# Where the score maxima are turned, constant stack rows, weight products, tables and padding rows in a macaron layer (two routed expert layers around one linear attention)

## The chip, the cores and the metric

The kernel runs on one core of one Trainium2 chip. The metric is the device time of one execution in microseconds (us). The kernel before was run three times: 2488.42, 2490.47 and 2494.25 us, median 2490.47 us.

## The reference

The input x has 8 batches of 512 tokens of 256 numbers (float32). Three sub-layers follow each other: an expert layer, a linear-attention layer, and the same expert layer again with the same weights.

```python
x = x + 0.5 * ffn(layernorm(x))
x = x + attention(layernorm(x))
x = x + 0.5 * ffn(layernorm(x))

def ffn(hs):                       # D = 256, 16 heads, 8 experts, top 2
    Q, K, V = hs@q_w+q_b, hs@k_w+k_b, hs@v_w+v_b      # 8 of each head's numbers are used
    attn = softmax(Q @ K.T / sqrt(8)); ao = attn @ V  # per batch and head, 512 x 512
    mla = ao @ o_w + o_b
    probs = softmax(mla @ router_w + router_b); topw, topi = top_k(probs, 2)
    h1 = gelu(mla @ w1[e] + b1[e]); h2 = h1 @ w2[e] + b2[e]
    return hs + 0.3 * sum over the two chosen e of weight * h2
```

The change lies in the expert layer, which runs twice; the attention layer between and the final combination are as they were.

## The kernel before

**Stages.** `load_and_make` loads small weights. Then `attend_and_apply_experts` runs for the first expert layer (tag f1), `attention_pass` (la), `attend_and_apply_experts` again (f2), and `combine` (fc). Each expert layer is three blocks with a barrier at the end of each: `attend_and_route` (softmax attention, router, and the scatter of each token's row into its two experts' regions of a DRAM table), `tile_tables` (21 VectorE steps that work out which expert each of 71 tiles belongs to, and beside them SP's load of the first half of w2 and of b2), and `experts` (71 tiles of 128 rows through w1, gelu and w2, with the second half of w2 loaded in its slot 1).

**Turns.** `attend_and_route` runs 11 turns over 8 batches, as a software pipeline. In one turn batch e has its scores, exponentials and weighted sums made ("e"), batch s = e+1 has its scores made once more to find row maxima ("s"), batch f = e+2 goes through the front (layer norm, q, k, v, "f"), and batch p = e-1 through the router and the scatter ("p"). The first turn has only f, the second s and f, the third e, s and f, turns 4 to 8 all four; the ninth has no f, the tenth e and p, the eleventh p alone. Turns 4 to 7 are in a hardware loop of two iterations with two turns each (`run_turns`), the others are written out. A turn has 16 groups (g = 0 to 15) of 4 score tiles; each engine's program is written out in this order, with front and router steps at fixed groups (tables FRONT and POST of each engine).

**The maxima.** Scores are computed from stacked bfloat16 parts: QS and KS hold, for every head, 6 products of parts in rows 0 to 47, zeros in rows 48 to 95, and in rows 96 to 98 the negated maxima (in QS) against ones (in KS). `score_for_max` (L749) makes a tile in one of three PSUM banks (SCM); VectorE's `maximum` (L501) reduces it. After 32 of the 64 tiles `split_maxima` (L508 to L511, four small VectorE operations) cuts the half's maxima into three parts, TensorE's `turn_maxima` (L758) turns them in the next SCM slot, and VectorE's `evacuate_mT` (L516) copies them out. The first half is split after g7 and turned after g8. The second half is split after g15 and turned at the very end of the turn. SP's `maxima` (L259, L261) writes them to DRAM, waits for that to land, and reads them back into rows 96 to 98; `score` (L768) of the next turn waits for it, for half 0 at its first tile and for half 1 at its 33rd.

**SP's order in a turn.** SP issues in program order: store of the residual, load of the next x, stores of the q and k parts (L276, L278), `maxima(s, 0)`, `stack_half(f, 0)`, `maxima(s, 1)`, `stack_half(f, 1)`. A `stack_half` (L253) is 12 DMAs of 64 KB, 8 partitions each, which lay the parts of half of the heads of batch f into QS and KS. It waits until the score tiles of batch e that read the same buffer are made. `score_for_max` of the next turn waits at its first tile for all 12 DMAs of half 0 (`half_loaded[0]`), and at its 33rd for those of half 1. TensorE works in order, so nothing behind such a wait runs.

**Beginnings.** GpSimd clears QS and KS and sets the ones with three memsets per buffer (`prepare_stacks`, L310, L311, L314), the first buffer before its part in the first turn, the second behind it. GpSimd also splits q and k into parts (`split`, L342 to L345, eight operations). In f1 TensorE multiplies o_w into w1 between turns one and two (`fold_weights`, L821 and L827, 8 experts), ScalarE evacuates.

**Ends.** After the last turn GpSimd's scatter of 8 indirect DMAs is followed by 8 more that write zero rows behind each expert's region (L386); then come the barrier, `tile_tables`, and another barrier.

Of the kernel before, what the change touches and what calls it, by code (L numbers as in the profile page):

```python
# [48 lines left out]

LN_STEPS = 6  # L50
# [33 lines left out]
def region_rows(tokens):  # L84
    return tokens + P


def attend_and_route(nc, new_sem, tag, nth, x_in, xr_out, xs, bank, ident, tri, w, scratch, routing, dims,
                     fold):
# [16 lines left out]
    K_MAX = 96  # L106
# [10 lines left out]
    PER_UNIT = SC + HALVES  # L117
# [3 lines left out]
    ROW, CW, start_row = routing["ROW"], routing["CW"], routing["start_row"]  # L121
# [4 lines left out]

    def max_slot(half):


        return (half + 1) * PER_HALF + min(HQ, SC - (half + 1) * PER_HALF) + half  # L130

    def score_slot(i):
        return i + sum(1 for half in range(HALVES) if i >= (half + 1) * PER_HALF + HQ)

    with ExitStack() as ctx:
# [38 lines left out]
        pad_f, pad_i = sb("pad_f", [P, E]), sb("pad_i", [P, E], I32)  # L174
# [12 lines left out]
        m3_ready, mT_filled = sem("m3_ready"), sem("mT_filled")  # L187
# [11 lines left out]
        dve_pads, carried, rows_out = sem("dve_pads"), sem("carried"), sem("rows_out")  # L199
# [5 lines left out]
        N_INIT = 9  # L205
        INIT = N_INIT * (nth + 1)

        SCE, SIDE, PVB, SCM = bank[0:2], bank[2:4], bank[4], bank[5:8]

        def run_turns(eng, turn, after_first=None, after_second=None, after_third=None):  # L210
            turn(None, None, START, None)
            if after_first is not None and fold is not None:
                after_first()
            turn(None, START, START + 1, None)
            if after_second is not None and fold is not None:
                after_second()
            turn(START, START + 1, START + 2, None)
            if after_third is not None and fold is not None:
                after_third()

            full = B - 3
            with eng.Fori(0, full // 2) as k:
                for odd in range(2):
                    b = k * 2 + (START + 1 + odd)
                    turn(b, b + 1, b + 2, b - 1, (START + 1 + odd) % 2)
            for b in range(START + 1 + full // 2 * 2, END + 1):
                turn(b if b < END else None, b + 1 if b + 1 < END else None,
                     b + 2 if b + 2 < END else None, b - 1)
# [6 lines left out]

        block = ctx.enter_context(nc.Block())

        @block.sync
        def _(sp):
# [3 lines left out]
            def stack_half(a, half, par, free):  # L243
# [20 lines left out]
            def turn(e, s, f, p, par=None):  # L264
                par_s, par_f = parity(s, 1, par), parity(f, 0, par)
# [15 lines left out]
                if f is not None:  # L281
                    if e is None:

                        sp.wait_ge(init, INIT if s is not None else INIT - 3)
# [9 lines left out]
            run_turns(sp, turn)  # L294
# [8 lines left out]
        def _(pool):  # L303
# [3 lines left out]

            def prepare_stacks(i, done):

                pool.memset(QS[i][0:K_MAX, :, :], 0.0).then_inc(init, 1)  # L310
                pool.memset(KS[i][0:K_MAX, :, :], 0.0).then_inc(init, 1)  # L311

                pool.wait_ge(init, INIT - N_INIT + done + 2)
                pool.memset(KS[i][K_MAX:K_EXP, :, :], 1.0).then_inc(init, 1)  # L314
                pool.wait_ge(init, INIT - N_INIT + done + 3)

# [3 lines left out]
            prepare_stacks(0, 3)  # L320
# [15 lines left out]
            def split(a):  # L336

                s = Steps(pool, pool_front, a, 6)
                wait(pool, split_stored, a * 32)
                for whole, rest, parts, ready, done in ((qf, qres, q3, q_ready, q3_ready), (kf, kres, k3, k_ready, k3_ready)):  # L340
# [23 lines left out]
            def turn(e, s, f, p, par=None):  # L364
# [5 lines left out]
                if s is None and p is None:  # L370

                    prepare_stacks(1, 6)

            def complete_biases():

# [7 lines left out]

            pool.wait_ge(pads_ready, nth + 1)
# [1548 lines left out]
```

## Time and profile before

| | |
|---|---|
| median of three runs | 2490.47 us |
| the profiled execution | 2496.27 us, its span 2494.6 us |
| f1: attend_and_route | from 14.0 us; first score tile at 79.1 us |
| f1: tables and experts | tables from 677.7 us, experts from 687.2 us |
| f2: attend_and_route | from 1523.4 us; first score tile at 1580.5 us |
| f2: tables | from 2184.0 us |
| busy, of the span | TensorE 79%, VectorE 62%, ScalarE 38%, GpSimd 26% |

Times are from the start of the span. A busy share is an average over stages: in the turns TensorE is busy about nine tenths of the time and VectorE over eight tenths, while at the starts and ends of the expert layers most engines wait. The profiled execution is 5.8 us above the median of the runs.

### The profile page before, as it was taken

Reading aid. Unit: us, or ns where it says so; the run is one execution under the profiler, and the core shown is the slowest. Engines: PE = TensorE matmul, PEld = TensorE weight load, DVE = VectorE, ACT = ScalarE, POOL = GpSimd, SP = SyncE. Lnnn points to the kernel's source line nnn. Section 1 sums busy time; section 2 is a strip of 40 time slices with the busy share of each in tenths; the row PEclk is TensorE's granted clock in tenths of the full one; section 3 lists DMA queues with packets and bytes.
Section 4 is the critical chain, followed back from the end, with each engine's and each line's share of the span. In section 5 each row is a group of like instructions: output and inputs, shape, how many; then the busy total and the mean of one; then the engine's idle time right before and its main releaser. Section 6 shows DMA issues by size and latency. Waiting matters only on the chain. (4 is left out here: it accounts for less than half of the span.)

```text
span 2494.6 us, 43922 instructions
## 1 busy us (share of the span) xinstructions
PE 1965.2 (79%) x12512; PEld 1086.7 (44%) x12513; DVE 1541.0 (62%) x3524; ACT 938.1 (38%) x1694; POOL 656.6 (26%) x674
## 2 busy tenths in 40 slices
PE   3898988898289959888889874599989898369940
PEld 2323333332079945655656563123333332069940
DVE  3688878885244436656666663588878885244433
ACT  1056556567122214322333321046555567212210
POOL 7422333221312231111100004522332321312246
PEclk9799999999689978888897886589998999779975
DMA  4333323220122231111011001332323230032236
GB/s 123 58 62 57 62 54 61 51 49 11 68 98 73 73 129 35 52 52 53 18 40 47 27 18 34 71 63 56 62 55 59 48 57 11 26 131 73 70 116 189
DMA packets 154273, 155.20 MB, mean 62 GB/s; under 512 B 19744, under 2 KB 144416, under 8 KB 153760
## 3 DMA queue, kind: packets, MB, share of 16 engines
q1 hardware_dynamic: 122912, 108.39, 19.1%
q0 software_dynamic: 10752, 26.23, 3.4%
q10 hardware_dynamic: 20448, 18.62, 2.1%
q8 instruction: 77, 1.26, 0.2%
q14 instruction: 84, 0.69, 0.1%
HBM read 90.80 MB, written 62.39 MB: 61 GB/s over the span
## 5 line engine op out<-in xcount | busy, mean ns | idle before, releaser
L501 DVE TENSOR_REDUCE f_M<-bank 128x1 f32<-128x512 f32 x1024 | 666.6, 684 | 222.1 <-PE bank L749 201.9
L435 ACT ACTIVATE f_PT<-bank 128x512 f32<-128x512 f32 x1024 | 574.9, 596 | 341.2 <-PE bank L768 330.7
L749 PE MATMUL bank<-f_KS,f_QS 96*128 96x512 bf16 x1024 | 424.8, 417 | 111.0 <-DVE f_M L501 79.3
L768 PE MATMUL bank<-f_QS,f_KS 99*128 99x512 bf16 x1024 | 402.5, 397 | 29.6 <-ACT f_PT L435 21.9
L778 PE MATMUL bank<-f_PT,f_V 128*32 128x512 f32 x2048 | 282.7, 627 | 0.0
L768 PEld LDWEIGHTS bank<-f_QS,f_KS 99*128 99x128 bf16 x1024 | 101.1, 100 | 395.6 <-ACT f_PT L435 268.3
L749 PEld LDWEIGHTS bank<-f_KS,f_QS 96*128 96x128 bf16 x1024 | 103.1, 101 | 262.7 <-DVE f_M L501 186.7
L1064 PE MATMUL bank<-f_w,f1m_gT 128*128 x568 | 136.2, 383 | 0.1
L1064 PE MATMUL bank<-f_w,f2m_gT 128*128 x568 | 135.9, 382 | 0.1
L357 POOL DMA_INDIRECT routed_rows<-f_AO,f_rows_i x128 | 124.2, 970 | 42.1 <-issue 42.1
L331 POOL TENSOR_TENSOR f_xr<-f_hs,f_half 128x1024 f32<-128x1024 f32 x16 | 30.3, 1893 | 301.7 <-DVE f_hs L81 268.8
L1064 PEld LDWEIGHTS bank<-f_w,f1m_gT 128*128 128x128 f32 x568 | 103.6, 193 | 11.8 <-issue 0.5
L1064 PEld LDWEIGHTS bank<-f_w,f2m_gT 128*128 128x128 f32 x568 | 103.6, 193 | 11.8 <-issue 0.5
L1000 ACT ACTIVATE f1m_gT<-f1m_hb 128x512 f32<-128x512 f32 x71 | 44.7, 630 | 158.8 <-DVE f1m_hb L1021 158.8
L1000 ACT ACTIVATE f2m_gT<-f2m_hb 128x512 f32<-128x512 f32 x71 | 44.7, 630 | 158.4 <-DVE f2m_hb L1021 158.4
L354 POOL TENSOR_TENSOR f_pool_carrier<-f_zero 128x1 f32<-128x1 f32 x16 | 3.1, 193 | 384.0 <-DVE f_rows_i L603 343.8
L1588 PE MATMUL bank<-la_o,la_attT 128*128 128x256 f32 x256 | 81.4, 473 | 16.1 <-ACT la_attT L1389 16.1
L1327 POOL TENSOR_TENSOR la_pool_carrier<-la_zero 128x1 f32<-128x1 f32 x8 | 1.5, 192 | 332.6 <-DVE la_idx L1418 332.6
L988 POOL COPY f1m_w1t<-folded_w 128x512 f32 x71 | 43.6, 614 | 170.8 <-PE bank L1053 154.1
L988 POOL COPY f2m_w1t<-folded_w 128x512 f32 x71 | 43.6, 614 | 170.4 <-PE bank L1053 154.0
L1516 DVE SCALAR_TENSOR_TENSOR la_sqk<-la_qk,la_low 128x512 f32<-128x512 f32 x64 | 41.4, 688 | 68.8 <-ACT la_low L1368 68.3
L1381 ACT ACTIVATE la_SS<-la_SS 128x512 f32<-128x512 f32 x32 | 20.1, 630 | 161.1 <-DVE la_SS L1463 161.1
(279 smaller groups left out, 3272.1 us busy)
## 6 DMA issues: line engine op xcount, KB each, us to landing
f_QS<-q_parts SPq DMA_DIRECT2D x192, 64.0 KB
f_KS<-k_parts SPq DMA_DIRECT2D x192, 64.0 KB
expert_rows<-f1m_y ACTq DMA_DIRECT2D x71, 128.0 KB, 1.7
expert_rows<-f2m_y ACTq DMA_DIRECT2D x71, 128.0 KB, 1.7
xr<-f_xr SPq DMA_DIRECT2D x16, 512.0 KB, 3.0
f_w<-in_L_ffn_w SPq DMA_DIRECT2D x4, 2048.0 KB, 8.2
q_parts<-f_q SPq DMA_DIRECT2D x16, 384.0 KB, 2.5
k_parts<-f_k SPq DMA_DIRECT2D x16, 384.0 KB, 2.5
```

The lines of the kernel that those rows point to most:

```text
L331: pool.tensor_tensor(XR[:, :, :], HS[:, :, :], half[:, :].unsqueeze(2).to_broadcast([P, T, D]), ALU.mult).then_inc(xr_half, 1)
L357: pool.indirect_dma_start(out=xs, out_offset=bass.IndirectOffsetOnAxis(ap=rows_i[:, t, n:n + 1], axis=0), in_=AO[par][:, t, :], in_offset= ...
L435: act.activation(PT[:, i % 8, :], SCE[i % 2][:, :], ACT.Exp).then_inc(probs_ready, 1)
L501: dve.tensor_reduce(M[:, t, h:h + 1], SCM[n % 3][:, :], AX.X, ALU.max).then_inc(scm_drained, 1)
L749: pe.matmul(SCM[n % 3][:, :], QS[par][0:K_MAX, h, t * P:(t + 1) * P], KS[par][0:K_MAX, h, :], start=True, stop=True).then_inc(scm_filled, 1)
L768: pe.matmul(SCE[i % 2][:, :], KS[par][0:K_EXP, h, t * P:(t + 1) * P], QS[par][0:K_EXP, h, :], start=True, stop=True).then_inc(sce_filled, 1)
L778: pe.matmul(PVB[hq * PV_W:(hq + 1) * PV_W, :], V[par][:, t, head(q, hq), :], PT[:, i % 8, :], start=(t == 0 and q % 2 == 0), stop=(t == T ...
L988: pool.tensor_copy(W1[:, buf, :], w["w1"][:, ds(e * F, F)]).then_inc(w1_ready, 1)
L1000: act.activation(GT[:, buf, :, :], Hb[:, buf, :, :], ACT.Gelu).then_inc(gT_ready, 1)
L1064: last = pe.matmul(OB[buf][:, 0:D], GT[:, buf, f, :], w["w2"][:, ds(e * (FC * D) + f * D, D)], start=(f == 0), stop=(f == FC - 1))
L1516: dve.scalar_tensor_tensor(sqk[par][:, i, :], qk[par][:, i, :], 0.0, low[:, i % 2, :], ALU.max, ALU.add).then_inc(sqk_ready, 1)
L1588: last = pe.matmul(OB[:, 0:D], attT[:, c, :], w["la_o"][:, c, :], start=(c == 0), stop=(c == KC - 1))
```

## The change

`attend_and_route` takes over the tables (`make_tables`) and the early load of w2; the block `tile_tables` is gone.

1. **Maxima.** Three small pieces spread over groups. Of batch s, half 0 is split at g12 (one of the four operations after each tile), turned after g13 and copied out at g14. Half 1 is left to the next turn, where the batch is e: split at g0, turned after g3, copied out at g4. Both use PSUM bank SIDE[1] in place of an SCM bank. `score_for_max` counts plain tiles.
2. **SP's order.** `maxima(e, 1)` stands first in a turn, `maxima(s, 0)` after the stores of q and k parts as before, then `stack_half(f, 0)` and `stack_half(f, 1)`.
3. **No loop.** All turns are written out.
4. **Constant rows.** ScalarE's queue issues, for each of two buffers, two DMAs that fill rows 48 to 95 from an SBUF row of zeros (about 0.79 MB each) and one that fills the ones. The memsets are gone. The 16 small loads of q_b move from SP's queue to ScalarE's.
5. **First batch.** q is split by VectorE, k by GpSimd; the KS half of the first stack (12 DMAs) is issued from ScalarE's queue.
6. **Weight products.** One expert's product at each even group of turn two and its bias products at each odd one, evacuated by ScalarE in the same groups.
7. **Ends.** Zero rows by plain DMAs, four from SP and four from ScalarE. The tables follow on VectorE in the same block, while GpSimd scatters. All of w2 (4 MB) is loaded by SP after turn three, b2 in slot 1 of `experts`, and `experts` waits for both.

```diff
@@ attend_and_route, constants
-    A_FRONT, A_SCM, A_POST = LN_STEPS, 3 * HALVES, 2 + 22
+    A_FRONT, A_SCM, A_POST = LN_STEPS, 3, 2 + 22
+    G_LAST, G_FIRST = 0, 12
@@ sync
                 for n, (i, j) in enumerate(TERMS):
...
-                    for to, source in ((QS[par], q_scr[i]), (KS[par], k_scr[j])):
+                    both = ((QS[par], q_scr[i]), (KS[par], k_scr[j]))
+                    for to, source in both[:1] if a == START else both:
@@
             def maxima(a, half, par):
-                sp.wait_ge(scm_drained, a * PER_UNIT + max_slot(half) + 1)
+                sp.wait_ge(mT_ready, a * HALVES + half + 1)
@@
             def turn(e, s, f, p, par=None):
+                if e is not None:
+                    maxima(e, 1, par_e)
                 if f is not None:
...
                 if s is not None:
                     maxima(s, 0, par_s)
                 if f is not None:
                     stack_half(f, 0, par_f, e * SC + SC // 2 if e is not None else None)
-                if s is not None:
-                    maxima(s, 1, par_s)
                 if f is not None:
                     stack_half(f, 1, par_f, (e + 1) * SC if e is not None else None)
+            run_turns(sp, turn, after_third=fetch_w2)
+            sp.wait_ge(pads_ready, nth + 1)
+            store_pads(sp, 0)
@@ gpsimd
-            prepare_stacks(0, 3)
+            pool.memset(zero_b[:, :], 0.0).then_inc(init, 1)
...
-            for e in range(E):
-                pool.indirect_dma_start(
-                    out=xs, out_offset=bass.IndirectOffsetOnAxis(ap=pad_i[:, e:e + 1], axis=0),
-                    in_=zero_rows[:, :], in_offset=None).then_inc(pads_stored, 16)
@@ scalar
+            def begin_folds():
+                act.wait_ge(split_stored, START * 32 + 32)
+                for half in range(HALVES):
+                    heads = slice(half * HH, (half + 1) * HH)
+                    for n, (i, j) in enumerate(TERMS):
+                        act.dma_start(KS[START % 2][n * KPH:(n + 1) * KPH, heads, :],
+                                      k_scr[j].rearrange("(h k) t -> k h t", k=KPH)[:, heads, :]).then_inc(half_loaded[half], 16)
...
+            for i in range(2):
+                for to in (QS[i], KS[i]):
+                    rows = slice(K_TERMS, K_MAX)
+                    act.dma_start(to[rows, :, :], zero_b[rows, :].unsqueeze(1).to_broadcast([K_MAX - K_TERMS, H, S])) \
+                       .then_inc(constant_rows[i], 16)
+                act.dma_start(KS[i][K_MAX:K_EXP, :, :].rearrange("p h (x y) -> p (h x) y", y=P),
+                              w["ones_b"][K_MAX:K_EXP, :].unsqueeze(1).to_broadcast([PARTS, H * S // P, P])) \
+                   .then_inc(constant_rows[i], 16)
@@ vector
-                dve.tensor_copy(mT[:, :], SCM[max_slot(half) % 3].bitcast(BF16)[0:PARTS * HH, 0:S]).then_inc(scm_drained, 1)
+                dve.tensor_copy(mT[:, :], SIDE[1].bitcast(BF16)[0:PARTS * HH, 0:S]).then_inc(mT_ready, 1)
@@
-                        if g == HH:
+                        if e is not None and g == G_LAST:
+                            split_maxima(e, 1, s_last, i % HQ)
+                        if s is not None and g == G_FIRST:
+                            split_maxima(s, 0, s_scm, i % HQ)
+                        if e is not None and g == G_LAST + 4 and i % HQ == 1:
+                            evacuate_mT(e, 1)
+                        if s is not None and g == G_FIRST + 2 and i % HQ == 0:
                             evacuate_mT(s, 0)
-                        if g % HH == HH - 1:
-                            split_maxima(s, g // HH, s_scm)
-                if s is not None:
-                    evacuate_mT(s, 1)
@@
+            dve.tensor_copy(pad_i[:, :], start_row[:, :]).then_inc(pads_ready, 1)
             s.end()
+            make_tables(dve)
@@ tensor
             def score_for_max(a, i, par):
+                if i == 0 and a < START + 2:
+                    pe.wait_ge(constant_rows[a % 2], CONSTANT)
...
+                    if fold is not None and e is None and s is not None:
+                        (fold_weight, fold_bias)[g % 2](g // 2)
+                    if e is not None and g == G_LAST + 3:
+                        pe.wait_ge(v_ready, min(e + 2, END) if isinstance(e, int) else e + 2)
+                        if p is not None:
+                            pe.wait_ge(ao_ready, (p + 1) * 2)
+                        turn_maxima(e, 1)
+                    if s is not None and g == G_FIRST + 1:
+                        if p is not None:
+                            pe.wait_ge(logits_ready, p + 1)
                         turn_maxima(s, 0)
...
-                if s is not None:
-                    turn_maxima(s, 1)
```

## Rows read from the trace of the kernel before

**Rows 1.** Windows: us, busy by engine (x), PE clock, DMA share, GB/s; turn four
```profile
196.00:263.00 67.00, 59.92 (x322) 21.55 (x321) 56.10 (x126) 40.90 (x75) 19.85 (x18) 0.97 0.32 59
```
**Rows 2.** Timeline of the start of f1: start us, us, engine line op
```profile
1.36 5.47 SPq L1796 DMA_DIRECT2D q_bs<-in_L_ffn_q_b  x16
...
18.77 9.59 DVE L645 COPY start_row<-region 128x8 f32<-128x8 f32 x1
...
30.25 5.08 DVE L484 TENSOR_SCALAR f_ve<-f_mv 128x4 f32<-128x4 f32 x1
...
38.07 1.97 PE L666 MATMUL bank<-ident,f_hs 128*128 128x128 f32 x8 [38.07 <-DVE f_hs L81]
...
79.14 0.81 PE L749 MATMUL bank<-f_KS,f_QS 96*128 96x512 bf16 x3
```
**Rows 3.** Timeline, the last two of the eight weight products in f1
```profile
72.14 1.96 PE L821 MATMUL bank<-w,owT 128*128 128x512 f32 x4
...
75.64 1.96 PE L821 MATMUL bank<-w,owT 128*128 128x512 f32 x4
```
**Rows 4.** Timeline of the start of f2
```profile
1546.08 1.97 PE L666 MATMUL bank<-ident,f_hs 128*128 128x128 f32 x8 [26.51 <-DVE f_hs L81]
...
1565.23 0.33 SPq L253 DMA_DIRECT2D f_QS<-q_parts  x1
...
1580.49 2.00 PE L749 MATMUL bank<-f_KS,f_QS 96*128 96x512 bf16 x4 [22.57 <-DMA f_KS<-k_parts]
```
**Rows 5.** Windows: the load of w1, and a stack on its way
```profile
22.00:24.00 2.00, 0.00 (x0) 0.00 (x0) 2.00 (x1) 0.00 (x0) 2.00 (x1) 1.00 0.99 365
...
1572.00:1574.00 2.00, 0.00 (x0) 0.00 (x0) 0.00 (x0) 0.00 (x0) 2.00 (x1) 0.50 0.59 61
```
**Rows 6.** Timeline of VectorE: V copied out, just behind a turn's first maximum
```profile
134.96 0.41 DVE L468 TENSOR_TENSOR f_V<-bank,v_b 128x256 f32<-128x256 f32 x1
...
196.89 0.41 DVE L468 TENSOR_TENSOR f_V<-bank,v_b 128x256 f32<-128x256 f32 x1
...
263.82 0.42 DVE L468 TENSOR_TENSOR f_V<-bank,v_b 128x256 f32<-128x256 f32 x1
...
536.23 0.41 DVE L468 TENSOR_TENSOR f_V<-bank,v_b 128x256 f32<-128x256 f32 x1
...
1636.83 0.41 DVE L468 TENSOR_TENSOR f_V<-bank,v_b 128x256 f32<-128x256 f32 x1
...
2042.36 0.41 DVE L468 TENSOR_TENSOR f_V<-bank,v_b 128x256 f32<-128x256 f32 x1
```
**Rows 7.** Timeline, turn four: half 0 of the maxima, first stack DMA, VectorE in g14
```profile
233.63 0.41 DVE L516 COPY f_mT<-bank 24x512 bf16<-24x512 bf16 x1
...
236.17 0.27 SPq L253 DMA_DIRECT2D f_QS<-q_parts  x1
...
253.50 3.08 DVE L501 TENSOR_REDUCE f_M<-bank 128x1 f32<-128x512 f32 x5
```
**Rows 8.** Windows, turn four: the stack of half 0 ends
```profile
246.00:248.00 2.00, 1.14 (x6) 0.31 (x4) 1.64 (x5) 1.61 (x3) 0.00 (x0) 1.00 0.57 59
248.00:250.00 2.00, 1.68 (x12) 0.48 (x13) 2.00 (x4) 0.05 (x1) 0.00 (x0) 1.00 0.42 46
```
**Rows 9.** Timeline of TensorE, turn six, g8; and a window after such a wait, turn five
```profile
370.84 0.39 PE L749 MATMUL bank<-f_KS,f_QS 96*128 96x512 bf16 x1 [1.73 <-DVE f_M L501]
...
300.00:304.00 4.00, 4.00 (x15) 0.95 (x8) 2.42 (x9) 2.27 (x5) 0.00 (x0) 0.50 0.33 111
```
**Rows 10.** Timeline of the end of attend_and_route, the tables, the first tiles of f1
```profile
661.02 0.19 POOL L362 TENSOR_TENSOR f_pool_carrier<-f_zero 128x1 f32<-128x1 f32 x1 [1.42 <-DMA routed_rows<-f_AO,f_rows_i]
...
670.54 0.96 POOL L386 DMA_INDIRECT routed_rows<-f_zero_rows,f_pad_i  x1 [0.30 <-issue]
...
677.69 0.40 SPq L1876 DMA_DIRECT2D f_w<-in_L_ffn_w  x1
...
687.17 1.28 ACT L1000 ACT_TABLE_LOAD   x1 [44.41 <-PEq L847]
...
699.89 3.62 PE L1064 MATMUL bank<-f_w,f1m_gT 128*128 x8
```

More of the change, by code:

```diff
@@ L120, in attend_and_route @@
     q_scr, k_scr, m_scr = scratch
-    ROW, CW, start_row = routing["ROW"], routing["CW"], routing["start_row"]
+    ROW, CW, start_row, tables, IDX = (routing[n] for n in ("ROW", "CW", "start_row", "tables", "IDX"))
+    NT = tables.shape[2]
+    REG, RUNGS, PAIRS = region_rows(B * S), B * S // P + 1, 2 * B * S // P
     def head(q, g):
         return q // 2 * HH + g * 2 + q % 2
[L127 to L133, printed above, removed]
     with ExitStack() as ctx:
@@ L211, in run_turns @@
             turn(None, None, START, None)
-            if after_first is not None and fold is not None:
+            if after_first is not None:
                 after_first()
             turn(None, START, START + 1, None)
-            if after_second is not None and fold is not None:
+            if after_second is not None:
                 after_second()
             turn(START, START + 1, START + 2, None)
-            if after_third is not None and fold is not None:
+            if after_third is not None:
                 after_third()
[L221 to L226, printed above, removed]
+            for b in range(START + 1, END + 1):
                 turn(b if b < END else None, b + 1 if b + 1 < END else None,
@@ L234, in parity, with room @@
             return unit % 2 if unit is not None else None
+        count, tiles, ends = sb("count", [P, E]), sb("tiles", [P, E]), sb("ends", [P, E])
+        spare = PT[:, :, :].rearrange("p i s -> p (i s)")
+        def room(at, shape):
+            n = int(np.prod(shape))
+            names = " ".join("abc"[:len(shape)])
+            return spare[:, at:at + n].rearrange(f"p ({names}) -> p {names}", **dict(zip("abc", shape)))
+        above = room(0, (E, RUNGS))
+        low, lower = sb("low", [P, E, E]), sb("total", [P, 1])
@@ L457, in _ @@
+            run_turns(act, turn, after_first=begin_folds, after_second=end_folds)
+            act.wait_ge(pads_ready, nth + 1)
+            store_pads(act, 1)
         @block.vector
@@ L829, in fold_weights, with fold_weight @@
-                last.then_inc(small_filled, 1)
+            def fold_weight(e):
+                if e % (E // 2) == 0:
+                    pe.wait_ge(fold["w1_loaded"][e // (E // 2)], 16)
+                wait(pe, fold_ready, e - 1)
+                for c in range(DC):
+                    last = pe.matmul(SCE[(e + 1) % 2][:, 0:F], fold["owT"][:, c, :], fold["w1"][:, e, c, :],
+                                     start=(c == 0), stop=(c == DC - 1))
+                last.then_inc(fold_filled, 1)
@@ L831, in release_folds, with fold_bias @@
+            def fold_bias(e):
+                for f in range(FC):
+                    at = 2 * E + e * FC + f
+                    for c in range(DC):
+                        last = pe.matmul(PVB[:, at:at + 1], fold["w1"][:, e, c, f * P:(f + 1) * P],
+                                         w["o_b"][:, c:c + 1], start=(c == 0), stop=(c == DC - 1))
+                if e == E - 1:
+                    last.then_inc(small_filled, 1)
             def release_folds():
+                if fold is None:
+                    return
```

321 lines of the change are left out of this document (155 added, 166 removed).

## The prediction

> **What bounds the kernel now.** I read the windows by stage first. In a full turn [rows 1] TensorE is busy 59.9 of 67 us and VectorE 56.1: both are near full and run in lockstep, so a wait of either costs its whole length, and an operation saved on one of them saves little. The timelines of the two starts come next [rows 2, 4]: 14.0 to 79.1 us pass in f1 and 1523.4 to 1580.5 in f2 before the first score tile. In f1 it waits for TensorE's weight products, in f2 for the stack (the releaser is the DMA into KS). On the way VectorE loses time to GpSimd's memsets: a copy of 8 numbers takes 9.59 us and a small scalar operation 5.08, against about 0.2 for such operations elsewhere. Then the ends [rows 10]. Last, as the change moves a point in SP's program, I read what SP does in a turn and how long its transfers take [rows 5, 7, 8]; that decides the forecast.
>
> **The stack gets a late start.** SP issues `stack_half(f, 0)` behind `maxima(s, 0)`, which waits for the copy of the turned maxima. Today that copy is at 233.63 in turn four, 30 us before the next turn's V copy at 263.82, and the first stack DMA goes out at 236.17, 2.5 us later (store, landing, load) [rows 6, 7]. The 12 DMAs end near 249.5, where the DMA share falls [rows 8]: 13.3 us, with room to spare. The change puts the copy behind the first tile of g14. VectorE's five maxima from 253.50 at 0.6 us each are the last of g13 and the four of g14, so the copy would start at 254.7, 9.1 us before the next V copy. From there: 2.5 us to the first stack DMA, the transfer, and 1.3 us (estimate: a tile, its maximum, the V copy). SP issues half 1 as soon as TensorE has made its last score tile, so both halves stand queued together, as at the start of f2, where the first tile comes 15.26 us after the first stack DMA [rows 4]. I take 15.2, since that row has both halves queued; 13.3 is the other end. The distance is then 2.5+15.2+1.3 = 19.0 us instead of 9.1: TensorE stands 9.9 us at the first `score_for_max` of the next turn, with only one score tile of e made, and VectorE and ScalarE stand with it. The half's own maxima load goes ahead of the stack and is no later bound; half 1 is needed some 35 us later and comes in time.
>
> **Turns, part by part.** (a) Taken away: the maxima's detour. At g8 TensorE waits 1.73 us [rows 9], because the four small split operations run beside GpSimd's split of k; at g12 they don't. With the wait for the turn itself 2.0 us in a full turn, about 1 in turns two and three. The wait at the old end of the turn (about 1 us) is swallowed by the new one. Bounds 0 and 3. (b) Added: after 10 us of idling TensorE's clock will be granted at the lower level. After a short wait it was: 0.50, that is 1.2 GHz, at 300 to 304 [rows 9]. The start of a turn is where VectorE has most to do, so I take 0.7 us a turn, estimated; bounds 0 and 3.5, for 15 matmuls in 4 us there against 19 on the average of rows 1, over 16 us. (c) The loop's return (some 2.7 us idle once per layer) and the slower half turns that follow g8's wait go: I count these by giving turns four to eight all turn four's length.
>
> A full turn was 263.82-196.89 = 66.9 us and becomes 66.9+9.9-2.0+0.7 = 75.5. Turn three was 61.9 and becomes 61.9+9.9-1+0.7 = 71.5. From turn three to the start of nine that makes 71.5+5x75.5 = 449 us, against 401.3 in f1 and 405.5 in f2 [rows 6]: +48 and +44. Turn two: its last two groups have no e work, so the copy is about 8.3 us before its end (estimate from 9.1), +10.7-1+0.7 = +10.4 in each layer. Turn nine gains 1.5 each: -3. Sum of the turns: +48+44+21-3 = **+110**.
>
> **Products inside turn two.** A product with its bias takes 3.50 us [rows 3], eight take 28. Turn two is bound by VectorE, and each group has room; but TensorE is in order, the three banks cover only about 1.8 us (three maxima at 0.6), and it starts at the lower clock. I take +8 us in turn two. Bounds: 0 (all hidden) and 28 (none).
>
> **Start of f1.** The q_b loads leave SP's queue: 16 issues, 5.5 us, of which 5.1 are gained (they run beside SP's nine on ScalarE's queue). Without memsets 9.59+5.08 becomes 0.4: 14.3 less. ScalarE issues six constant DMAs ahead of its layer-norm steps: +1 (estimate; bounds 0 and 5, if its queue backs up). The turned HS moves from 38.07 to 19.7. From there to the first stack DMA it was 19.15 us [rows 4]; k no longer waits behind q on GpSimd (about 2.3 less): 16.9. First stack DMA at 36.6, first score tile 15.2 later at 51.8 instead of 79.14: **-27.3**.
>
> **Start of f2.** Block start to HS becomes 10.8 us as in f1 (38.07-14.0-14.3+1): 1534.2 instead of 1546.08, -11.9, and -2.3 for k: **-14.2**. The second buffer's memsets (20.8 us on GpSimd) hid behind the stack and save nothing.
>
> **Two queues for the first stack.** While a stack is on its way the DMA share is 0.59 in all 2 us stretches, though up to 24 DMAs are queued, and 61 GB/s move; the load of w1 has 0.99 and 365 [rows 5]. If two queues filled the rest, half 0 would take 15.2x0.59 = 9 us, 6 less per layer. More queued work did not raise the share, so I take no gain; 6 stays as the bound. The Trainium skill (DMA: Bandwidth & Descriptors, the section on why a DMA increments its semaphore by 16) says that a copy is spread over the largest number of engines up to 16 that divides the slowest dimension on both sides, here 8 partitions and so 8 engines, the same whichever queue issues it. By it the sum stands as it is; by the other reading it is 12 less.
>
> **Ends.** The last scatter has landed at 661.02; the eight zero-row writes follow, the last issued by 671.5 and landed some 1.4 later; 4.8 us after that the tables' block begins, and lasts to 687.17 [rows 10]. After: tables (9 us) and plain DMAs run during the 12 us of scatters, from 649. The exit of 4.8 us stays. That is 672.9-661.0 = 11.9 and 687.2-677.7 = 9.5, 21.4 in all. The first w2 matmul comes 12.7 us after the block's start; without w2's load before tile 2's rows I estimate 3.8 less (bounds 0 and 5; b2 of 1 MB is still loaded there and now gates TensorE too). -25 per layer, **-50**. The 4 MB of w2 in turn four follow the stack on SP's queue, about 11 us at the rate of rows 5, and are through before or shortly after half 1's maxima are stored; these have over 10 us to spare: 0, bound +8 per layer.
>
> **Sum.** -27.3-14.2+8+110-50 = +26.5. The span 2494.6 becomes 2521, the execution 2496.3 becomes 2523; it lies 5.8 over the median, so the median becomes 2490.5+26.5 = **2517 us**.
>
> **Rivals.** (1) The stack is less late: 13.3 us instead of 15.2 in 14 turns (-27) and two queues help (-12): 2478, faster. For it: the row of turn four, measured alone; against it: both halves are queued now. (2) The stack isn't what the next turn waits for, or the copy comes early enough. Then 12 turns save 2 to 3 us instead of gaining 9, and turn two too: about -150 from the sum, 2366. For it stands only that I read SP's order by hand. (3) The clock: each wait of 10 us leaves TensorE at 1.2 GHz well into the turn, 3.5 us in each of 14 turns instead of 0.7, +39: 2556. For it: rows 9, where TensorE is busy all 4 us and makes fewer tiles. It decides once the low stretch lasts beyond some 8 us. (4) The starts don't shrink: the constant rows (3.2 MB) and w1 (4.2 MB) share the DMA engines, and ScalarE blocks while it issues; +15, 2532. In f1 both need about 20 us at the rate of rows 5, from 10 to 31, before the stack at 36.6: against it.
>
> **Chances.** Forecast 0.57, (1) 0.20, (2) 0.04, (3) 0.13, (4) 0.06. A measurement tells a difference from none at about 0.2%, 5 us. Faster: most of (1), (2) and a tail of the forecast: 0.23. Same: where (1) holds in part, 0.09. Slower: 0.68. The forecast's own range is 2495 to 2540, from the bounds of the products, (a) and the starts taken together; with (1), (3) and (4) it becomes 2470 to 2552, and leaves out (2) and the outer ends.
>
> **What the profile will show.** The first `score_for_max` of turns three to nine preceded by some 10 us of idle TensorE, released by a stack DMA; the V copies 75 us apart in turns four to eight; the first stack DMA 2.5 us behind the copy in g14; the DMA share still near 0.6; the first score tile near 52 us, and 43 us after f2's block start; turn two of f1 about 8 us longer than that of f2; the experts' block beginning 5 us after the last scatter has landed and not 26. I am wrong if the V copies lie under 68 us apart, or if the starts and ends save much less than 90 us together.

## The result, and the profile after

The changed kernel takes 2534.98 us (median of 4 runs, 2531.19 to 2536.12) against 2492.25 (2488.42 to 2494.25) for the kernel before: ratio 1.0171, 95% interval 1.0153 to 1.0188. It is slower by 43 us. The two profiled executions differ by less, 2529.5 against 2494.6 of span, +34.9; the accounting below is of these two.

The page of the changed kernel, its span and three of its costliest groups (columns: busy us, mean ns | idle us before, what ended most of it):

```profile
span 2529.5 us, 41513 instructions
...
L577 DVE TENSOR_REDUCE f_M<-bank 128x1 f32<-128x512 f32 x1024 | 674.5, 685 | 342.8 <-PE bank L847 332.7
L487 ACT ACTIVATE f_PT<-bank 128x512 f32<-128x512 f32 x1024 | 575.5, 596 | 442.4 <-PE bank L864 437.3
L847 PE MATMUL bank<-f_KS,f_QS 96*128 96x512 bf16 x1024 | 420.9, 417 | 207.6 <-DMA f_KS<-k_parts 141.2
```

`score_for_max` is now L847. It waits 141.2 us for the DMA that loads the stack, and ScalarE's exponentials (L487) and VectorE's maxima (L577) stand with it. One of these waits in detail, at the end of turn five of f1, as the timelines of VectorE, SP and TensorE have it (answers to [rows 6, 7]):

```profile
338.26 0.40 DVE L596 COPY f_mT<-bank 24x512 bf16<-24x512 bf16 x1
...
340.94 0.27 SPq L314 DMA_DIRECT2D f_QS<-q_parts  x1
...
356.17 0.61 PE L847 MATMUL bank<-f_KS,f_QS 96*128 96x512 bf16 x1 [10.44 <-DMA f_KS<-k_parts]
...
357.43 0.42 DVE L545 TENSOR_TENSOR f_V<-bank,v_b 128x256 f32<-128x256 f32 x1
```

Copy, 2.7 us to the first stack DMA, 15.2 us to the first tile, 1.3 us to the V copy: 19.2 us, of which TensorE idles 10.44. The windows of that turn, of its wait and of what follows (columns as in [rows 1]):

```profile
283.36:357.43 74.07, 60.14 (x322) 21.58 (x321) 53.76 (x128) 40.68 (x75) 21.16 (x20) 0.91 0.28 56
346.00:357.00 11.00, 0.83 (x2) 0.28 (x3) 0.18 (x1) 0.65 (x2) 1.59 (x2) 0.64 0.58 82
357.00:362.00 5.00, 5.00 (x15) 2.24 (x14) 4.86 (x14) 2.99 (x5) 0.19 (x1) 0.50 0.58 68
...
361.00:365.00 4.00, 4.00 (x22) 1.85 (x21) 3.93 (x14) 2.20 (x5) 0.00 (x0) 0.78 0.58 62
365.00:369.00 4.00, 3.97 (x22) 1.25 (x20) 3.86 (x11) 2.99 (x6) 0.00 (x0) 1.00 0.25 28
```

Behind the wait the granted clock is 0.50, then 0.78 between 361 and 365, and 1.00 from 365 on.

The start of f1, timeline of ScalarE's queue and the first score tile (answers to [rows 2]):

```profile
10.34 0.76 ACTq L525 DMA_DIRECT2D f_QS<-f_zero_b  x1
11.13 0.67 ACTq L525 DMA_DIRECT2D f_KS<-f_zero_b  x1
11.84 1.69 ACTq L527 DMA_DIRECT2D f_KS<-ones_b  x1
13.56 4.39 ACTq L525 DMA_DIRECT2D f_QS<-f_zero_b  x1
17.98 4.84 ACTq L525 DMA_DIRECT2D f_KS<-f_zero_b  x1
22.85 7.97 ACTq L527 DMA_DIRECT2D f_KS<-ones_b  x1
30.87 0.20 ACT L72 ACTIVATE f_lg<-f_ve 128x4 f32<-128x4 f32 x1 [20.02 <-issue]
...
65.24 1.98 PE L847 MATMUL bank<-f_KS,f_QS 96*128 96x512 bf16 x4 [7.87 <-DMA f_KS<-k_parts]
```

The second column is how long one issue held the queue. The second buffer's three hold ScalarE for 17 us, so its layer-norm step, whose input had been ready since 16.4, starts at 30.87.

The end of f1, timelines of GpSimd, ScalarE and TensorE (answers to [rows 10]):

```profile
707.61 0.19 POOL L421 TENSOR_TENSOR f_pool_carrier<-f_zero 128x1 f32<-128x1 f32 x1 [1.40 <-DMA routed_rows<-f_AO,f_rows_i]
...
713.36 1.28 ACT L1044 ACT_TABLE_LOAD   x1 [24.24 <-PEq L136]
...
722.53 2.89 PE L1108 MATMUL bank<-f_room,f1m_gT 128*128 x8
```

Where the 34.9 us are, by V copies, block starts and first w2 matmuls (us; stages in the order of time):

| stage | before | after | change | forecast |
|---|---|---|---|---|
| f1, to the first V copy | 80.2 | 66.5 | -13.7 | -27.3 |
| f1, turn two (products inside) | 54.8 | 75.1 | +20.3 | +18.4 |
| f1, turns three to eight | 401.3 | 438.0 | +36.7 | +48 |
| f1, turn nine to the first w2 matmul | 163.7 | 143.0 | -20.6 | -26.5 |
| f2, block start to the first V copy | 58.4 | 49.7 | -8.7 | -14.2 |
| f2, turn two | 55.1 | 61.0 | +5.9 | +10.4 |
| f2, turns three to eight | 405.5 | 440.6 | +35.0 | +44 |
| f2, turn nine to the first w2 matmul | 164.0 | 143.1 | -20.9 | -26.5 |
| all else, not touched | | | +0.9 | 0 |

### The profile page after: what moved, and what is told of

It reads as the page before. It is cut to its first block and busy times, and to the rows that moved or that the text cites. A ratio compares the mean times of both kernels' runs of the same rounds, so it can differ in the third digit from the quotient of the medians.

```text
span 2529.5 us, 41513 instructions
## 1 busy us (share of the span) xinstructions
PE 1945.5 (77%) x12512; PEld 1085.4 (43%) x12513; DVE 1489.0 (59%) x3530; ACT 938.0 (37%) x1694; POOL 551.6 (22%) x640
## 5 line engine op out<-in xcount | busy, mean ns | idle before, releaser
L577 DVE TENSOR_REDUCE f_M<-bank 128x1 f32<-128x512 f32 x1024 | 674.5, 685 | 342.8 <-PE bank L847 332.7
L487 ACT ACTIVATE f_PT<-bank 128x512 f32<-128x512 f32 x1024 | 575.5, 596 | 442.4 <-PE bank L864 437.3
L847 PE MATMUL bank<-f_KS,f_QS 96*128 96x512 bf16 x1024 | 420.9, 417 | 207.6 <-DMA f_KS<-k_parts 141.2
L864 PE MATMUL bank<-f_QS,f_KS 99*128 99x512 bf16 x1024 | 408.2, 403 | 38.9 <-ACT f_PT L487 27.5
L874 PE MATMUL bank<-f_PT,f_V 128*32 128x512 f32 x2048 | 272.2, 605 | 0.0
L847 PEld LDWEIGHTS bank<-f_KS,f_QS 96*128 96x128 bf16 x1024 | 104.3, 103 | 342.9 <-DMA f_KS<-k_parts 126.4
L1108 PE MATMUL bank<-f_room,f1m_gT 128*128 x568 | 135.4, 382 | 0.1
L1108 PE MATMUL bank<-f_room,f2m_gT 128*128 x568 | 135.0, 381 | 0.1
L1108 PEld LDWEIGHTS bank<-f_room,f1m_gT 128*128 128x128 f32 x568 | 103.3, 192 | 11.7 <-issue 0.5
L1108 PEld LDWEIGHTS bank<-f_room,f2m_gT 128*128 128x128 f32 x568 | 103.0, 191 | 11.6 <-issue 0.5
L1560 DVE SCALAR_TENSOR_TENSOR la_sqk<-la_qk,la_low 128x512 f32<-128x512 f32 x64 | 41.4, 689 | 68.7 <-ACT la_low L1412 68.2
L1702 PE MATMUL bank<-la_hsT,la_q 128*128 128x512 f32 x128 | 73.6, 728 | 9.9 <-ACT la_hsT L1398 9.9
```

The costliest lines, as they stand in the source:

```text
L487: act.activation(PT[:, i % 8, :], SCE[i % 2][:, :], ACT.Exp).then_inc(probs_ready, 1)
L577: dve.tensor_reduce(M[:, t, h:h + 1], SCM[(a * SC + i) % 3][:, :], AX.X, ALU.max).then_inc(scm_drained, 1)
L847: pe.matmul(SCM[(a * SC + i) % 3][:, :], QS[par][0:K_MAX, h, t * P:(t + 1) * P], KS[par][0:K_MAX, h, :], start=True, stop=True).then_inc(s ...
L864: pe.matmul(SCE[i % 2][:, :], KS[par][0:K_EXP, h, t * P:(t + 1) * P], QS[par][0:K_EXP, h, :], start=True, stop=True).then_inc(sce_filled, 1)
L874: pe.matmul(PVB[hq * PV_W:(hq + 1) * PV_W, :], V[par][:, t, head(q, hq), :], PT[:, i % 8, :], start=(t == 0 and q % 2 == 0), stop=(t == T ...
L1108: last = pe.matmul(OB[buf][:, 0:D], GT[:, buf, f, :], w["w2"][:, ds(e * (FC * D) + f * D, D)], start=(f == 0), stop=(f == FC - 1))
```

## The experiments

### Is it SP's order? e1, and again as e12

```diff
@@ sync, turn
-                if s is not None:
-                    maxima(s, 0, par_s)
                 if f is not None:
                     stack_half(f, 0, par_f, e * SC + SC // 2 if e is not None else None)
+                if s is not None:
+                    maxima(s, 0, par_s)
```

> The changed kernel with one thing turned round in SP's program: the first half of the next stack is issued before maxima(s, 0) and not behind it. Theory A (the stack's load starts late because it is queued behind the copy that moved to g14): in turn five the rows of k are stored at 319.86, 36.5 us after the turn's V copy, so the first stack DMA goes out at about +39 and has landed by +54, before the end of a turn of some 64 us. The waits of the first score_for_max, 141.2 us in the page, fall below 10, the V copies of full turns stand 63 to 65 us apart instead of 73 to 74, and the time falls by 14 waits of 9 to 10 us, to about 2400 us (ratio to the kernel before 0.96 to 0.97). Rival B (the stack's transfer itself is what is long, since 24 DMAs share 8 partitions' queues whatever their order, or it is k's split that is late): the waits only shrink by a third, the time stays above 2480. Rival C (the wait moves: maxima of half 0, now stored behind the stack's issues, come late for the first score of the next turn): a new wait of L864 on the maxima's DMA of some 5 us a turn, about 2460.

Measured: 2387.37 us (2382.7 to 2388.03), ratio to the kernel before 0.957 (0.9553 to 0.9588), 148 less than the changed kernel. Timeline of SP in turn four:

```profile
227.84 0.36 SPq L341 DMA_DIRECT2D k_parts<-f_k  x1
...
230.43 0.29 SPq L314 DMA_DIRECT2D f_QS<-q_parts  x1
```

The windows of turn five:

```profile
254.60:318.00 63.40, 58.18 (x322) 20.37 (x323) 53.92 (x128) 40.54 (x76) 21.52 (x21) 1.00 0.33 65
```

The stack goes out as soon as k's rows have landed, 24 us before the next V copy (254.58). Of the waits for the stack in turns three to nine none is left, and turns four to eight take 63.2 to 63.5 us where the changed kernel takes 73.4 to 74.6. Over the 14 late stacks the gain is 10.5 us each. Theory A holds and B falls. C's wait shows in one place only, turn two of f2, where the maxima's store goes out at 1568.38 behind the stack, their load 6.7 us later, and the first score tile of e stands 3.3 us:

```profile
1577.64 0.38 PE L864 MATMUL bank<-f_QS,f_KS 99*128 99x512 bf16 x1 [3.34 <-issue]
```

In the full turns that load follows 1.4 us behind its store and nothing waits for it. So the order of two calls in SP's program costs 148 us. e12 is the same kernel in more rounds, beside e11.

> The kernel with only the stack's first half issued ahead of the maxima, once more and in more rounds, on the chip of e11: 2387 within 5 us; it is the measure for e11, and with it for whether the order alone explains the loss: ratio to the kernel before 0.957.

Measured: 2386.55, ratio 0.9588 (0.9569 to 0.9607).

### The same wait, by the place of the copy: e2, e3

```diff
-    G_LAST, G_FIRST = 0, 12
+    G_LAST, G_FIRST = 0, 10
```

(8 in e3.)

> The changed kernel with G_FIRST = 10 instead of 12: the split, the turn and the copy of the first half's maxima come two groups earlier, the copy behind the first tile of g12. SP's order stays as in the change. Two groups of a full turn are about 8.5 us. Theory A: the wait of the first score_for_max falls by that, from 9.9 to 1 to 2 us per turn, and the turns are 65 to 67 us; time about 2535 - 14 x 8 = 2420. Rival B (the length of the transfer or k's split sets the wait, not where the copy stands): waits and time stay within 20 us of the changed kernel, 2515 to 2535. A further cost could show: the split's small operations fall into groups 10 to 12 where VectorE compares and ranks experts; at most 1 us a turn, +14.

> The same with G_FIRST = 8: the copy behind the first tile of g10, four groups or 17 us earlier than in the change. Theory A: 17 is more than the wait, so nothing of it is left and the gain over the run with g12 is only the 1 to 2 us a turn that remained there: 2400 to 2415. If each group earlier went on paying 4.3 us a turn, the time would be 2535 - 14 x 17 = 2297; theory A excludes that. Rival D (a turned-maxima wait at g9 as the kernel before had at g8, since the small operations again stand beside GpSimd's split of k): TensorE waits 1.7 to 2 us a turn at g9, and the time is 25 us above that of the run with g12's remaining wait gone, about 2430.

Measured: 2447.01 (0.98; 0.9765 to 0.9834) and 2408.55 (0.9672; 0.965 to 0.9695). Timelines of VectorE and TensorE of e2, from the copy to the next turn:

```profile
315.79 0.40 DVE L596 COPY f_mT<-bank 24x512 bf16<-24x512 bf16 x1
...
333.02 0.61 PE L847 MATMUL bank<-f_KS,f_QS 96*128 96x512 bf16 x1 [3.44 <-DMA f_KS<-k_parts]
```

The next V copy is at 334.28, 18.5 us behind the maxima's copy. So the chain of copy, issue and transfer keeps its length (18.4 to 19.5 in the changed kernel), and a wait remains only as far as the rest of the turn is shorter. In e2 3.4 us remain, more than the 1 to 2 expected, because the two groups are not 8.5 us long but 6.7: e1 has its copy 8.3 us before the V copy, and e2, its wait taken off, 15.0. With the copy at g10 the distance is 22.8 and no wait for the stack is left in the turns. e3 is still 21 us behind e1: its turns take 64.6 to 66.9 us. Its TensorE, in one such turn, waits 2.7 us for exponentials and 2.9 for maxima, no wait for a maximum longer than 0.7, so rival D's wait of 1.7 to 2 us at g9 isn't there. One wait for an exponential is long, and it comes back in each of turns four to eight:

```profile
363.60 0.39 PE L864 MATMUL bank<-f_QS,f_KS 99*128 99x512 bf16 x1 [2.39 <-ACT f_PT L487]
```

Just before it ScalarE waits 2.8 us for a router step of VectorE (`f_L`), where it is 1.6 in e1, and pieces of the split stand among VectorE's steps there. In e1's turns no wait for an exponential is over 2 us. How much of the 21 us this makes was not tried.

### The start: e4, e9, e8, e11

e4 moves one thing in the changed kernel:

```diff
@@ scalar
+            def constants(i):
+                for to in (QS[i], KS[i]):
...
             def begin_folds():
+                constants(1)
                 act.wait_ge(split_stored, START * 32 + 32)
@@
-            for i in range(2):
-                for to in (QS[i], KS[i]):
...
+            constants(0)
             run_turns(act, turn, after_first=begin_folds, after_second=end_folds)
```

> The changed kernel with one thing moved: the three constant-row DMAs of the second stack buffer are issued by ScalarE behind its work of turn one (before it waits for the first stack), not ahead of its layer-norm steps. Theory A (ScalarE is blocked while it issues: in f1 the six DMAs hold it from 10.34 to 30.82, and its layer-norm step starts at 30.87 although its input is ready from 16.4): the first three are issued by 13.6, the layer-norm step starts at 16.5, the first score tile of f1 comes at 51 to 53 instead of 65.24, and in f2 some 7 us earlier than 48.4 after the block's start; the time falls by 18 to 21, to 2514 to 2517. Rival E (the load of w1 and the constants share the DMA engines, and what waits is the data): the first score tile moves by under 5 us because the stack, q_bs or the second buffer's constants arrive behind w1; time above 2528.

Measured: 2524.24 (2521.7 to 2528.64), ratio 1.0129 (1.0109 to 1.0149), 11 us less. Timelines of ScalarE, SP and TensorE at the start of f1:

```profile
16.54 0.20 ACT L72 ACTIVATE f_lg<-f_ve 128x4 f32<-128x4 f32 x1 [5.76 <-DVE f_ve L564]
...
33.82 2.21 SPq L341 DMA_DIRECT2D k_parts<-f_k  x1
...
45.22 4.14 SPq L314 DMA_DIRECT2D f_QS<-q_parts  x12
...
60.18 1.98 PE L850 MATMUL bank<-f_KS,f_QS 96*128 96x512 bf16 x4 [8.29 <-DMA f_KS<-k_parts]
```

Both theories hold in part. The layer-norm step comes 14.3 us earlier, as A had it, but k's rows, 0.4 MB, take 11.4 us to land where it is 2.5 in a turn, and only 5 us arrive at the first tile. The next two runs ask what is in their way. e9 is e4 with w1's load behind the first stack, e8 is e1 with the second buffer's constants in g9 of turn two.

> The changed kernel with the second buffer's constant rows behind turn one's work (2524.24) and with w1's load (4.2 MB) issued by SP behind the first stack instead of ahead of turn one. It is there to see the start without w1 on the DMA engines, not to be faster: turn two's products then wait for w1. Theory A (k's rows land late because w1 shares the engines): they land 2.5 us after they are issued, the first stack DMA goes out at 36 to 37 and the first score tile comes at 51 to 52, as my prediction had it; turn two becomes 5 to 15 us longer, time 2515 to 2530. Rival (the constants alone, or something in q and k, hold the stack up): first stack DMA after 42.

> The kernel with the first half of the stack issued ahead of the maxima (2387.37), and with the three constant-row DMAs of the second buffer issued by ScalarE in g9 of turn two instead of ahead of its layer-norm steps. With those DMAs behind turn one's work, where w1 was still on its way, ScalarE was free at 13.5 but k's rows took 11.4 us to land and the first stack DMA went out at 45.22, 11 us before the other form but 8.6 later than my 36.6. Theory A (two causes, ScalarE's issues and the shared DMA engines): without 1.6 MB of constants among the start's 7.9 MB the engines are free some 4 to 8 us earlier, the first stack DMA of f1 goes out at 37 to 41 and the first score tile comes at 52 to 56; f2 gains 7. Turn two has slack for ScalarE, so its length stays within 2 us. Time 2387 - 10 to 13 - 7 = 2367 to 2370. Rival (only ScalarE's issues count, or w1 alone fills the engines until 42): first score tile at 60, time 2376. Rival (issuing in g9 blocks ScalarE and with it the products, or slows the stack of the second buffer): turn two 5 to 10 us longer, time 2378 to 2387.

Measured: 2535.84 (1.0177; 1.0122 to 1.0232) and 2380.45 (0.9545; 0.951 to 0.958). f1's start in four kernels, us:

| | k's rows issued | landed in | first stack DMA | first tile |
|---|---|---|---|---|
| changed kernel | 48.17 | 2.5 | 50.70 | 65.24 |
| e4: constants 1 behind turn one's work | 33.82 | 11.4 | 45.22 | 60.18 |
| e9: and w1 behind the stack | 33.89 | 8.5 | 42.43 | 57.50 |
| e8: w1 first, constants 1 in g9 of turn two | 33.09 | 7.1 | 40.15 | 55.17 |

Either load alone (e9 the constants, e8 w1) keeps k's rows on their way for 7 to 8.5 us instead of 2.5, and both together for 11.4. So e9's theory A is wrong: w1 isn't the only thing in the way. In the changed kernel ScalarE's block hid this: the DMA share is 0.96 from 42 to 46 and 0.32 from 46 to 50, and k's rows go out at 48.17. In e9 turn two takes 88.1 us; its first product waits 15.7 us for w1.

In e8 the starts gain 10.4 and 7.4 us, but turn two takes 68.2 and 58.6 instead of 64.1 and 53.4. SP's queue in f1 shows how the two transfers meet:

```profile
92.92 0.36 SPq L341 DMA_DIRECT2D k_parts<-f_k  x1
95.44 0.29 SPq L314 DMA_DIRECT2D f_QS<-q_parts  x1
95.77 2.16 SPq L314 DMA_DIRECT2D f_KS<-k_parts  x1
97.97 1.80 SPq L314 DMA_DIRECT2D f_QS<-q_parts  x1
```

ScalarE issues the constants at 94.29, a microsecond before SP issues the second stack; an issue of it then takes some 2 us instead of 0.3. In f2 this reaches TensorE. The maxima's store goes out at 1562.21 and the load behind it at 1573.43, as SP waits 10.9 us for the store to land, and the first score tile of e stands 8.09 us instead of e1's 3.34:

```profile
1573.43 0.24 SPq L322 DMA_DIRECT2D f_QS<-m_parts  x1
1575.91 0.58 PE L868 MATMUL bank<-f_QS,f_KS 99*128 99x512 bf16 x1 [8.09 <-issue]
```

These 4.8 us are nearly all of the 5.2. In f1 it doesn't: TensorE waits for no DMA in turn two. The windows of that turn in e8, e1 and, for the kernel of e1 once more, e12:

```profile
56.40:124.56 68.16, 64.83 (x263) 35.34 (x263) 45.41 (x91) 8.80 (x17) 13.36 (x12) 0.78 0.35 77
66.82:130.95 64.13, 59.75 (x263) 33.86 (x263) 45.50 (x90) 8.79 (x17) 13.38 (x12) 0.85 0.30 56
66.96:128.55 61.59, 57.46 (x263) 33.02 (x263) 45.39 (x90) 8.79 (x17) 13.38 (x12) 0.89 0.31 58
```

The same matmuls keep TensorE busy 5.1 us longer in e8 than in e1, at a granted clock of 0.78 instead of 0.85, and one and the same kernel (e1, e12) differs there by 2.5 us with the clock. So the 4.1 us of f1 aren't shown to come from the constants. e11 puts the constants into g1.

> The kernel with the first half of the stack issued ahead of the maxima, and with the second buffer's three constant-row DMAs issued by ScalarE in g1 of turn two (in g9 they cost turn two 4.1 us in f1 and 5.2 in f2, against 10.4 gained at f1's start and 7.4 at f2's). Theory A (in g9 their 1.6 MB stood in the way of k's rows and of the second stack; in g1 only the half stack for g8 is on its way, with over 20 us to spare): the starts keep their gain and turn two stays within 1 us of 64.1 and 53.4: 17 us under the same run's time of e12, about 2370. Rival (ScalarE's blocked issuing or the products' evacuations in turn two are what costs): turn two 4 to 5 us longer again, 8 to 9 us under e12. A stage the change does not touch (linear attention) moved by 7 us with the granted clock between two of these kernels, so a difference under 5 us tells nothing.

Measured: 2370.76 us (2366.93 to 2371.62), ratio 0.9521 (0.9508 to 0.9534), 15.8 under e12 on the same chip. The first V copy of f1 is at 55.74 (e12: 66.96), turn two takes 61.7 and 53.5 us (61.6 and 52.8). By its numbers theory A holds; of its reason, the constants in the way of the transfers, only the part in f2 is shown (there the first score tile's wait is 3.3 us again). This is the version that beats both kernels: 4.8% under the kernel before, 6.5% under the changed one.

### The products: e5

```diff
@@ tensor, begin_folds (and evacuate_fold(e) likewise on scalar)
+                for e in range(E):
+                    fold_weight(e)
+                    fold_bias(e)
@@ tensor, turn
-                    if fold is not None and e is None and s is not None:
-                        (fold_weight, fold_bias)[g % 2](g // 2)
```

> The changed kernel with the eight weight products of f1 put back between turns one and two, as in the kernel before; all else as changed. In the changed kernel turn two of f1 takes 75.1 us and that of f2 61.0, so the products cost 14 us inside the turn (8 were forecast). Between the turns they take some 28 us of TensorE from about 57 on (its first product can begin when owT is copied), but it would stand until 65.2 anyway for the stack. Theory A (a product inside the turn costs half of what it costs ahead of it): the first score tile moves from 65.24 to 85 to 87, turn two falls to 61, the sum is +6 to +8, time about 2542. Rival (products in the turn hide nothing, the 14 us are another cost of turn two in f1, such as w1's or w2's transfers): turn two stays above 70 and the time is 2555. Rival (they hide entirely behind the stack's load when made early): time 2521 to 2525, and the part of the change that moves them in costs time.

Measured: 2553.69 us, spread over 2539.32 to 2570.86, ratio 1.0238 (1.0167 to 1.0308). Timeline of TensorE, what stands before the products and the last product:

```profile
54.87 1.02 PE L919 MATMUL bank<-router_w,owT 128*128 128x8 f32 x4 [9.68 <-ACT owT L507]
...
104.38 3.76 PE L930 MATMUL bank<-f_room,owT 128*128 128x512 f32 x4
107.94 3.41 PE L938 MATMUL bank<-o_b,f_room 128*128 128x1 f32 x16
111.21 1.98 PE L847 MATMUL bank<-f_KS,f_QS 96*128 96x512 bf16 x4
```

Two of the five windows over the products:

```profile
60.00:70.00 10.00, 10.00 (x36) 7.78 (x35) 0.00 (x0) 1.20 (x2) 0.00 (x0) 0.50 0.57 71
...
100.00:110.00 10.00, 10.00 (x33) 7.16 (x31) 0.00 (x0) 1.20 (x2) 0.00 (x0) 0.50 0.00 0
```

The first tile comes at 111.21, 46 us later and not 20, and turn two falls to 64.0. A product takes 6.83 us here (111.21 less 104.38) and 3.50 in [rows 3]: the granted clock is 0.50, that is 1.2 GHz, from the first product to the last, over 54 us in which TensorE never idles. In the kernel before the products follow other work directly and run at the full clock; here 9.7 us of idle time stand before them. That is one execution. The four took 2539, 2543, 2565 and 2571 us: two lie where theory A had them (2542), and two, among them the profiled one, some 27 us above, about what eight products at 3.3 us more would cost. Whether they ran at the full clock in the first two isn't shown, as only one execution has a trace. So the direction of theory A is right, and its price held for two executions and was far too low for the others; moving the products in is worth 19 us by the medians and 34 by the two spans. Turn two of f1 is still 2.5 us longer than that of f2 without products (64.0 and 61.5), which the rival (another cost of turn two in f1) may claim.

### The queues: e10

```diff
@@ sync, stack_half (and the twelve KS DMAs go from scalar)
-                    for to, source in both[:1] if a == START else both:
+                    for to, source in both:
```

> The kernel with the first half of the stack issued ahead of the maxima (2387.37), and with all 24 DMAs of the first stack on SP's queue, as in the kernel before, instead of half of them on ScalarE's. Theory A (the transfer keeps a share of 0.58 of the DMA engines whichever queue issues it): from the first stack DMA to the first score tile it takes 14.5 to 15.5 us as now, and SP's longer issuing (8.3 instead of 4.1 us) hides behind the transfer; time within 3 us of 2387. Rival (two queues fill the engines better, the bound of 6 us a layer in my prediction): 20 to 21 us from the first stack DMA to the first tile, time 2395 to 2400.

Measured: 2391.4 (0.9608; 0.9567 to 0.9648), 4 us over e1, whose interval (0.9553 to 0.9588) overlaps with this one. First stack DMA, last one and first tile:

```profile
49.69 0.34 SPq L314 DMA_DIRECT2D f_QS<-q_parts  x1
...
58.95 2.08 SPq L314 DMA_DIRECT2D f_KS<-k_parts  x1
...
64.51 1.98 PE L841 MATMUL bank<-f_KS,f_QS 96*128 96x512 bf16 x4 [18.59 <-DMA f_KS<-k_parts]
```

14.8 us on one queue, 14.5 on two in the changed kernel: theory A. The Trainium skill (DMA: Bandwidth & Descriptors, "Issuing engines are not separate DMA queues") says the same, that several issuing engines save only the time of issuing, and the run agrees: SP's 11.3 us of issuing (49.69 to 61.03, against 4.1 for half of it in the changed kernel) hid behind the transfer.

## Why the prediction was right, and where it wasn't

2517 was forecast, with 2495 to 2540 as the forecast's own range and 2470 to 2552 in all; 2535 was measured, slower by 43 and not by 26.5. Its main step, that the stack starts late, is shown by e1 to e3. By one of its own two signs of being wrong it failed: starts and ends were to save some 90 us together and saved 64, turn nine included. Point by point:

- **The stack gets a late start.** Forecast: 2.5 + 15.2 + 1.3 = 19.0 us from copy to V copy, 9.9 of waiting. Measured 19.2 and 10.44. That both halves stand queued and take 15.2, not 13.3, was right, so rival (1) falls, and with e10 its two queues too.
- **Turns, (a) and (b).** Full turns were forecast at 75.5 and took 73.4 to 74.6. Without the wait they take 63.3 (e1), 3.6 under the 66.9 of before; I had taken 2.0 for the detour at g8 and counted the turn's old end of about 1 us apart. That term was too small, beyond its bound of 3 if the end belongs to it. (b), 0.7 for the clock, is about right: a stalled turn is 10.1 to 11.2 longer than e1's, with 10.4 of waiting in the row above. Rival (3) falls for the turns: its bound took 16 us at the lower clock, and after the wait that ends at 356.17 the clock is full again by 365. T3 to T8 came to +72 instead of +92, turn two of f2 to +5.9 instead of +10.4.
- **Products inside turn two.** +8 forecast. Turn two of f1 is longer than that of f2 by 14.0 in the changed kernel, and by 10.7 (e4), 10.7 (e1), 8.8 (e12) and 8.2 (e11). So the term is 8 to 14, of which 2.5 stay without the products (e5). It goes with the granted clock of f1's turn two: 0.80 in the changed kernel, 0.85 in e1, 0.89 in e12, which is the kernel of e1.
- **Starts.** This is the step that failed: "ScalarE issues six constant DMAs ahead of its layer-norm steps: +1 (estimate; bounds 0 and 5, if its queue backs up)". It was 14.3 in f1 by e4, where the layer-norm step stood free, and 7.7 in f2. The other terms of f1's start came as forecast: without memsets the copy of 8 numbers and the small scalar operation take 0.17 us each, and from the turned HS (33.57) it is 17.1 us to the first stack DMA (forecast 16.9) and 14.5 more to the first tile (15.2). And "In f1 both need about 20 us at the rate of rows 5, from 10 to 31" was wrong too: the two together move at some 200 GB/s at first and not at 365, and k's rows would have met them (11.4 us, e4). In e4's f2 they met too: k's rows took 8.5 us to land, and the first tile came only 0.4 us earlier, counted from the block's start. The two starts gave -22.4 instead of -41.5. Rival (4), with 0.06, had the mechanism and nearly the size (+15; it was +19), and its reason against, that all is over by 31, is what e4 refutes.
- **Ends.** Forecast 21.4 + 3.8 per layer. From the last scatter's landing to the first w2 matmul it is 14.9 us in f1 instead of 38.9, -24.0. The block exit takes 5.8 instead of 4.8, and from the block's start to that matmul it is 9.2 instead of 12.7. Turn nine to the scatter's landing was to gain 1.5 and lost 3.3; f2 shows the same sum. So of the 6 us missing per layer 1.2 are behind the scatter and 4.8 before its end. The late stack isn't their cause: from turn nine's V copy to the experts' block it is 133.0 us in e1 and 133.9 in the changed kernel. What their cause is was not tried.
- **w2 in turn four.** 0 forecast; turn four takes 73.4 and 73.6 us, the turns behind it 73.5 to 74.6. Right.

Too much was expected of the starts (by 19) and the ends (by 12), too little of the turns' own gain (by 29, turn two included), too little paid for the products (6). These nearly cancel: the sum of +26.5 stands against +34.9 by the spans. That the total came so close is in good part luck; the late stack, the largest term, was not. The other 8 us to the medians' 43 are the two profiled executions, one above its median and one below.

## What to carry to other kernels

When a wait is moved to a later place, list everything behind it in the same in-order program, above all in the queue that issues DMAs: here a change that is worth 4.1 to 4.3% with two calls turned round (e12, e1) lost all of it to one transfer queued behind one late wait. Issue first what has the longest transfer and the earliest ready input. And a DMA that replaces a memset isn't free to its issuer: a few large ones ahead of a critical step hold the issuing engine, and small latency-bound stores meet their data on the DMA engines; put them where neither is needed (e11).

## What was not expected of the hardware

- The first three constant DMAs of ScalarE (1.6 MB) are issued in 0.7 to 1.7 us each; the next three take 4.4 to 8.0 each while the first are on their way. The same three in e9, issued at 28.48 when little else is queued, take 0.69, 0.67 and 1.87.
- While the constants and w1 move together, at 18 to 22 in the changed kernel, the DMA share is above 1 and only 203 GB/s move, against 365 for w1 alone [rows 5] and 223 for the constants with the load of x (e9, 14 to 18):

```profile
18.00:22.00 4.00, 0.00 (x0) 0.00 (x0) 0.00 (x0) 0.00 (x0) 0.00 (x0) 1.00 1.26 203
```

- TensorE stayed at 1.2 GHz for over 54 us of unbroken work in e5's profiled execution. So the clock needn't return as soon as the engine is busy again, though behind the wait at 356 it did within 9 us; what lets it return isn't shown by these runs.
- From the last expert tile of f1 to the start of f2, which no edit touches, e8 took 7 us more than e1, with 0.83 against 0.90 of granted clock in one window of 100 us. A difference of a few us between two profiled executions says nothing here.
